# Linear attention and best-two router of a two-layer kernel: value sums with 17-column weights, query features as weights, and match_replace for the two best gates

## The reference

```
q, k, v = x Wq + bq, x Wk + bk, x Wv + bv          # 16 heads of 8
q', k'  = (elu(q R) + 1) / 16, (elu(k R) + 1) / 16 # R: 8 x 32, so 32 features a head
kv      = sum over tokens of k'^T v                # 32 x 8 a head
ksum    = sum over tokens of k'                    # 32 a head
out     = (q' kv) / max(q' ksum, 1e-6)             # then out Wo + bo
gate    = softmax(x Rt)                            # 8 experts; the 2 best are kept
gate    = gate / (sum of the kept + 1e-6)
y       = x W^T + b + sum over experts of gate_e (x A_e^T) B_e^T
```

## Time and profile before

| | us |
|---|---|
| median of three runs | 512.2 |
| the profiled execution | 512.39 |
| its span | 510.6 |
| PE busy | 469.4 |
| DVE busy | 380.0 |
| ACT busy | 241.8 |
| POOL busy | 104.0 |

### The profile page before, as it was taken

How to read it: one execution, slowest core, us unless ns; L and a number is a source line. 1 busy time by engine, 2 the same in 40 slices (tenths; PEclk the granted TensorE clock), 3 DMA queues, 4 the chain that set the end, 5 groups by cost and what they waited for, 6 DMA issues and landing times. The chain is left out here.

```text
span 510.6 us, 8076 instructions
## 1 busy us (share of the span) xinstructions
PE 469.4 (92%) x2949; PEld 233.9 (46%) x2949; DVE 380.0 (74%) x984; ACT 241.8 (47%) x340; POOL 104.0 (20%) x100
## 2 busy tenths in 40 slices
PE   8799989999999999998999899989989998987873
PEld 3332232333433443332435566575656656565552
DVE  6298887887888889879755987854876697664653
ACT  2404746666686665655783122722363236327210
POOL 9790153402480001000010002000200020031020
PEclk9999989999999999999999999968997999899877
DMA  4755342222132243310032113110220011000000
GB/s 154 242 144 186 95 130 94 95 72 80 42 114 95 71 115 106 108 29 13 10 85 57 68 62 104 43 41 20 76 70 22 22 62 42 1 22 0 2 21 21
DMA packets 24867, 36.18 MB, mean 71 GB/s; under 512 B 2678, under 2 KB 16246, under 8 KB 24822
## 3 DMA queue, kind: packets, MB, share of 16 engines
q1 hardware_dynamic: 24828, 35.67, 23.7%
HBM read 23.94 MB, written 11.53 MB: 69 GB/s over the span
## 5 line engine op out<-in xcount | busy, mean ns | idle before, releaser
L1106 DVE TENSOR_REDUCE negmax<-psum 128x1 f32<-128x512 f32 x256 | 170.1, 687 | 37.6 <-PE psum L506 37.4
L810 ACT ACTIVATE probs<-psum 128x1024 f32<-128x1024 f32 x128 | 127.5, 1022 | 62.0 <-PE psum L522 59.8
L506 PE MATMUL psum<-KS,QS 125*128 125x512 bf16 x256 | 99.9, 391 | 8.0 <-DVE negmax L1106 3.6
L541 PE MATMUL psum<-probs,VA 128*32 128x256 f32 x1024 | 81.0, 392 | 0.4 <-ACT probs L810 0.4
L522 PE MATMUL psum<-QS,KS 128*128 128x512 bf16 x256 | 76.5, 382 | 0.3
L789 PE MATMUL psum<-xT,late 128*128 128x512 f32 x144 | 74.0, 639 | 0.0
L506 PEld LDWEIGHTS psum<-KS,QS 125*128 125x128 bf16 x256 | 24.8, 97 | 83.2 <-DVE negmax L1106 39.7
L434 POOL TENSOR_SCALAR var<-mv 128x4 f32<-128x4 f32 x16 | 3.6, 225 | 278.9 <-DVE mv L1006 278.8
L929 ACT ACTIVATE QS<-psum 128x512 f32<-128x512 f32 x36 | 21.6, 599 | 60.1 <-PE psum L789 60.1
L1257 DVE SCALAR_TENSOR_TENSOR QS<-QS,psum 128x512 f32<-128x512 f32 x36 | 24.5, 679 | 31.3 <-ACT QS L929 31.3
L776 PEld LDWEIGHTS psum<-late,QS 128*128 128x128 f32 x288 | 36.6, 195 | 14.9 <-issue 7.3
(11 more groups left out here) (140 smaller groups left out, 568.6 us busy)
## 6 DMA issues: line engine op xcount, KB each, us to landing
stack_dram<-parts SPq DMA_DIRECT2D x24, 384.0 KB, 3.6
cw<-w_dram SPq DMA_DIRECT2D x32, 256.0 KB, 3.2
KS<-stack_dram SPq DMA_DIRECT2D x16, 288.0 KB
QS<-stack_dram SPq DMA_DIRECT2D x16, 288.0 KB
late<-in_late SPq DMA_DIRECT2D x6, 330.5 KB, 4.5
res<-in_x SPq DMA_DIRECT2D x4, 256.0 KB, 3.6
w_dram<-wT SPq DMA_DIRECT2D x4, 256.0 KB, 4.3
out_y<-KS SPq DMA_DIRECT2D x4, 256.0 KB, 2.3
```

Source lines behind the costliest of these rows:

```text
L506: mm(sm_bank(u)[:, :], QS[b % 2][0:KROW, h, qt * P:(qt + 1) * P], KS[b % 2][0:KROW, h, :], start=True, stop=True).then_inc(sm_full, 1)
L541: last_ = mm(ps[6][32 * j:32 * j + 32, q], VA[b % 2][:, kt, h, :], probs[:, n % 2, j, q], start=(kt == 0 and half == 0), stop=(kt == NT - ...
L810: fn(probs[:, n % 2, 2 * hf:2 * hf + 2, :], psum[:, 2 * hf:2 * hf + 2, :], ACT.Exp, scale=float(DH) ** -0.5).then_inc(exp_done, 1)
L1106: V.tensor_reduce(out=negmax[:, G % 4, i:i + 1], in_=sm_bank(u)[:, :], axis=X, op=ALU.max, negate=True).then_inc(sm_free, 1)
```

## The change

V moves from place 6 to 4, Q's steps 2 and 3 from 7 to 6. VK holds, for each pair of heads, 16 values and a column of ones. In KV these 17 columns are the weights, in the four column tiles of the array (one for each group of four heads), and 64 feature columns stream: 32 calls. ACT copies the 128 columns of the sums (kvt), KT transposes them in one go, and DVE writes KVB with 32 masked value columns and 4 masked sum columns a group. O takes a token tile of q features as 128-column weights and streams the 36 columns of KVB; two steps of eight calls, each for two token tiles. Its result has tokens first, with outputs and denominators beside each other, so OT, its ACT copies and the tile OU's use here go. DVE floors, inverts and multiplies once for each step of O. Everything from AT on moves one place forward. KT gets bank 4 behind the experts; Y2 keeps 6, Y1 keeps 4.

The router takes MAX8 of the exponentials into the places 6 to 13 of `top8`, whose places 0 to 5 hold -1, so that places 0 to 7 are six times -1 and the two best; match_replace writes 0 for those two, and the difference to the exponentials is what is kept. The division by the softmax sum is folded into the last one.

```diff
-KVW = HW + 1
+KVW = 2 * DH + 1
+OW = HW + HG
...
-        VK = sb("VK", [P, NT, NG, KVW])
-        KVB = sb("KVB", [P, 2, NG, HW])
+        VK = sb("VK", [P, NT, 2 * NG, KVW])
+        kvt = sb("kvt", [P, P])
+        KVB = sb("KVB", [P, NG, OW])
...
+        top8 = sb("top8", [P, NT, 14])
...
-        steps = ((0, "chunk", 0), (1, "norm1", 0), (3, "x2T", 0), (4, "kp", 0), (4, "qp", 0), (5, "K", 0), (5, "K", 1),
-                 (5, "K", 2), (5, "K", 3), (6, "V", 0), (6, "Q", 0), (6, "Q", 1), (7, "Q", 2), (7, "Q", 3), (7, "KV", 0),
-                 (8, "O", 1), (8, "O", 0), (9, "OT", 1), (9, "OT", 0), (10, "AT", 0), (11, "Y1", 0), (12, "norm2", 0),
-                 (14, "x3T", 0), (15, "lg", 0), (17, "ghT", 0), (18, "Y2", 0), (19, "norm3", 0))
+        steps = ((0, "chunk", 0), (1, "norm1", 0), (3, "x2T", 0), (4, "kp", 0), (4, "qp", 0), (4, "V", 0), (5, "K", 0),
+                 (5, "K", 1), (5, "K", 2), (5, "K", 3), (6, "Q", 0), (6, "Q", 1), (6, "Q", 2), (6, "Q", 3), (7, "KV", 0),
+                 (8, "KT", 0), (8, "O", 0), (8, "O", 1), (9, "AT", 0), (10, "Y1", 0), (11, "norm2", 0),
+                 (13, "x3T", 0), (14, "lg", 0), (16, "ghT", 0), (17, "Y2", 0), (18, "norm3", 0))
...
-                    "V": (vk_done, b + 1), "KV": (kvb_done, b + 1), "O": (sums_done[c % 2], b + 1),
-                    "OT": (floor_done, b + 1) if c else (attn_done, NB * NT + b + 1),
+                    "V": (vk_done, b + 1), "KV": (kvt_done, b + 1), "KT": (kvb_done, b + 1), "O": (attn_done, NB * NT + 2 * b + c + 1),
...
-                if kind == "OT":
-                    pe.wait_ge(sums_done[m], b + 1)
-                if kind == "O" and m == 1:
+                if kind == "KT":
+                    pe.wait_ge(kvt_done, b + 1)
+                if kind == "O" and m == 0:
...
-                    for c in range(4):
-                        for t in range(NT):
-                            last_ = mm(cols(c, KVW), KF[:, t, c * P:(c + 1) * P], VK[:, t, c, :],
-                                       start=(t == 0), stop=(t == NT - 1))
+                    for t in range(NT):
+                        for r in range(2):
+                            for c in range(NG):
+                                at = c * P + 64 * r
+                                last_ = mm(o[32 * c:32 * c + KVW, 64 * r:64 * (r + 1)], VK[:, t, 2 * c + r, :],
+                                           KF[:, t, at:at + 64], start=(t == 0 and r == 0), stop=(t == NT - 1),
+                                           tile_position=(0, 32 * c), skip_group_check=True)
+                if kind == "KT":
+                    last_ = tr(cols(0), kvt[:, :], ident)
                 if kind == "O":
 
-                    for c in range(NG):
-                        last_ = mm(o[HW * c:HW * (c + 1), :], KVB[:, m, c, :], QF[:, b % 2, c, :],
-                                   start=True, stop=True, tile_position=(0, HW * c))
-                if kind == "OT":
-
-                    for t in range(NT):
-                        v = OU[:, 0, m, t * P:(t + 1) * P]
-                        if m:
-                            last_ = mm(cols(t, H), v, ident[:, 0:P:DH], start=True, stop=True)
-                        else:
-                            last_ = tr(cols(t), v, ident)
+                    for t in range(2):
+                        for c in range(NG):
+                            last_ = mm(cols(NG * t + c, OW), QF[:, b % 2, c, (2 * m + t) * P:(2 * m + t + 1) * P], KVB[:, c, :],
+                                       start=True, stop=True)
...
-                if kind == "O":
+                if kind == "KV":
                     wait_full(act, u)
                     if a:
-                        wait_full(act, ("OT", a - 1, m))
-                    fn(OU[:, 0, m, :], bank_of(u)[:, :], ACT.Copy).then_inc(sums_done[m], 1)
+                        wait_full(act, ("KT", a - 1, 0))
+                    fn(kvt[:, :], bank_of(u)[:, 0:P], ACT.Copy).then_inc(kvt_done, 1)
...
-                tot = rl[:, 3, 0:NT]
-                yield from after(V.reduce_sum(tot, e, X))
-                yield from after(V.reciprocal(tot, tot))
-                yield from after(tt(gate8[:, :, :], e, tot.unsqueeze(2).to_broadcast([P, NT, E1]), ALU.mult))
-                m8 = r3(5, 8, rl)
+                tot, picked = rl[:, 3, 0:NT], rl[:, 4, 0:NT]
+                rest, best = r3(5, E1, rl), r3(6, E1, rl)
                 for t in range(NT):
-                    ins = V.max(m8[:, t, :], gate8[:, t, :])
+                    ins = V.max(top8[:, t, 6:14], e[:, t, :])
                 yield from after(ins)
-                yield from top(rl, gate8[:, :, :], m8, 2, E1, 6, "reset8")
-                yield from after(tt(gate8[:, :, :], gate8[:, :, :], r3(6, E1, rl), ALU.mult))
-                yield from after(V.reduce_sum(tot, gate8[:, :, :], X))
-                yield from after(V.tensor_scalar(tot, tot, 1e-6, None, ALU.add))
-                yield from after(V.reciprocal(tot, tot))
-                yield from after(tt(gate8[:, :, :], gate8[:, :, :], tot.unsqueeze(2).to_broadcast([P, NT, E1]), ALU.mult))
+                V.reduce_sum(tot, e, X)
+                for t in range(NT):
+                    ins = V.match_replace(out=rest[:, t, :], in_to_replace=top8[:, t, 0:8], in_values=e[:, t, :], imm_value=0.0)
+                yield from after(ins)
+                yield from after(tt(best, e, rest, ALU.subtract))
+                yield from after(V.reduce_sum(picked, best, X))
+                yield from after(V.scalar_tensor_tensor(out=picked, in0=tot, scalar=1e-6, in1=picked, op0=ALU.mult, op1=ALU.add))
+                yield from after(V.reciprocal(picked, picked))
+                yield from after(tt(gate8[:, :, :], best, picked.unsqueeze(2).to_broadcast([P, NT, E1]), ALU.mult))
...
-                if kind == "KV":
+                if kind == "KT":
                     wait_full(dve, u)
                     if a:
-                        wait_full(dve, ("O", a - 1, 0))
-
-                    kv = bank_of(u)[:, 0:NG * KVW].rearrange("p (c k) -> p c k", k=KVW)
+                        wait_full(dve, ("O", a - 1, 1))
+
+                    kv = bank_of(u)[:, 0:P].rearrange("p (c k) -> p c k", k=32)
                     own = c_["mask"].unsqueeze(1).to_broadcast([P, NG, HW])
-                    tt(KVB[:, 1, :, :], own, kv[:, :, HW:KVW].to_broadcast([P, NG, HW]), ALU.mult)
-                    tt(KVB[:, 0, :, :], kv[:, :, 0:HW], own, ALU.mult).then_inc(kvb_done, 1)
+                    tt(KVB[:, :, HW:OW], kv[:, :, 2 * DH:KVW].to_broadcast([P, NG, HG]), own[:, :, 0:HW:DH], ALU.mult)
+                    tt(KVB[:, :, 0:HW].rearrange("p c (r k) -> p c r k", r=2),
+                       kv[:, :, 0:2 * DH].unsqueeze(2).to_broadcast([P, NG, 2, 2 * DH]),
+                       c_["mask"].rearrange("p (r k) -> p r k", r=2).unsqueeze(1).to_broadcast([P, NG, 2, 2 * DH]),
+                       ALU.mult).then_inc(kvb_done, 1)
                     step(8)
-                if kind == "OT" and m == 1:
+                if kind == "O":
                     wait_full(dve, u)
-
-                    V.tensor_scalar(rt[:, 20, :], bank_of(u)[:, 0:NT * H], 256e-6, None, ALU.max).then_inc(floor_done, 1)
-                    step(1)
-                    dve.wait_ge(floor_done, a + 1)
-                    link(V.reciprocal(rt[:, 21, :], rt[:, 20, :]))
-                if kind == "OT" and m == 0:
-                    wait_full(dve, u)
-                    if a >= 2:
+                    if a >= 2 and m == 0:
                         wait_full(dve, ("AT", a - 2, 0))
-                    tt(attn[:, a % 2, :, :].rearrange("p t (h d) -> p t h d", d=DH),
-                       bank_of(u)[:, :].rearrange("p (t h d) -> p t h d", t=NT, d=DH),
-                       rt[:, 21, :].rearrange("p (t h) -> p t h", h=H).unsqueeze(3).to_broadcast([P, NT, H, DH]),
-                       ALU.mult).then_inc(attn_done, 1)
-                    step(8)
+
+                    v = bank_of(u)[:, 0:2 * NG * OW].rearrange("p (g k) -> p g k", k=OW)
+                    floor, inv = (rt[:, i, 32 * m:32 * (m + 1)].rearrange("p (g h) -> p g h", h=HG) for i in (20, 21))
+                    link(V.tensor_scalar(floor, v[:, :, HW:OW], 256e-6, None, ALU.max))
+                    link(V.reciprocal(inv, floor))
+                    tt(attn[:, a % 2, 2 * m:2 * m + 2, :].rearrange("p t (c h d) -> p (t c) h d", h=HG, d=DH),
+                       v[:, :, 0:HW].rearrange("p g (h d) -> p g h d", d=DH),
+                       inv.unsqueeze(3).to_broadcast([P, 2 * NG, HG, DH]), ALU.mult).then_inc(attn_done, 1)
+                    step(4)
...
+            link(V.memset(top8[:, :, :], -1.0))
```

17 lines of the change are left out of this document (8 added, 9 removed).

## The result

The changed kernel takes 523.29 us (median of 4 runs, 519.18 to 525.75) against 512.75 for the kernel before beside it (511.38 to 518.55): a ratio of 1.0204, 95% interval 1.0159 to 1.0249. It is slower, as forecast, but by 10.5 us and not by 4.3, just past the end of the range (523). A ratio here is taken over executions within 1.5% of the fastest of their kernel, so it is not quite the ratio of the medians. The profiled execution took 525.75 us and is the slowest of the four; its span is 523.0 [before: 510.6, rows 1].

What follows compares the result with a forecast made beforehand. TensorE, busy for 92% of the span, with its clock and the waits on its in-order queue, was taken as the bound. The terms -2.5 - 0.2 + 3.5 + 4.0 - 0.5 = +4.3 us on 512.2 gave 516.5 us, range 506 to 523.

Steps and rivals of the forecast that it cites:

- KV: Value sums on PE: 1.4 us at full clock in place of 3.49, saving 2.1 us a batch, 8.4 in all.
- The rival that the tiles don't overlap: KV's column tiles: 3.4 us in place of 1.4, +2.0 in each of four batches, 524.5 us; chance 0.06.
- O and KT: PE work per batch: new O 3.5 us, KT 0.11, against 3.3 for old O and OT; +0.3, 1.2 in all.
- The KT wait: Beside the experts, O stalls for KVB on VectorE: 1.75 us in each of three batches, +5.2 us; bounds 0 and 3.
- The lg wait: Router logits wait for K's passes on bank 6: 1.3 us in batch 1 (as before), 2.3 in batch 2 (+1.0).
- The down projection's waits: In batch 0, the down projection before O waits 1.8 us for its hidden tile.
- -2.5 - 0.2 + 3.5 = +0.8: Beside the experts: batch 0 gains 2.5 us, batch 1 gains 0.2, batch 2 loses 3.5.
- Batch 0: Slots 14 to 18: gain of 6.1 us at full clock, 1.2 with O at half clock; 2.5 taken.
- the tail: Last batch (3): O starts 1.8 us later behind x2T, z 2.2 us longer behind O; +4.0 us, bounds +1 and +7.
- Router: Shorter chain for the two best gates gives nothing in the last batch; with z's norm wait, -0.5 us taken.
- The rival with half clock in every batch: O at half clock: 3.3 us for each of batches 1 and 2, 2.5 more in the tail; 522.5 us; chance 0.12.

Runs made afterwards that it cites:

- e3: The changed kernel with each step of layer 2 back at the places of the kernel before (V at 6, Q2 and Q3 at 7): 517.47 us, ratio 1.0120.
- e4: The changed kernel plus warming matmuls in the last batch alone, ahead of K2, Q2, KT and O: 515.51 us, ratio 1.0028.
- e1: The kernel before with the new router chain for the two best gates alone: 513.53 us, ratio 1.0005.
- e2: The kernel before with the new KV, kvt and KT alone, O and OT as before: 503.68 us, ratio 0.9811.
- e5: The kernel before with the new O alone, old KV, masks in the new form: 521.94 us, ratio 1.0164.
- e7: The changed kernel with only AT to norm3 put one place later, as before; V and Q stay early: 517.31 us, ratio 1.0080.
- e13: The kernel before with new KV, masks early on VectorE and new O, plus lg's banks taken in turn: 506.74 us, ratio 0.9886.
- e6: The changed kernel with lg and its second half taking the next banks in turn beside the experts: 520.67 us, ratio 1.0170.
- e14: The kernel before with new KV, early masks, new router, last-batch warming and the rule of lg's banks in turn: 492.74 us, ratio 0.9604.
- e15: The kernel before with new KV, early masks, new router, last-batch warming, lg's banks in turn and new O: 500.09 us, ratio 0.9745.
- e8: The kernel before with new KV alone and VectorE writing the masks KVB at KV's place in its list: 494.51 us, ratio 0.9657.

## Why the prediction was right in its direction and wrong in its size

**KV: right, the gain even larger.** 1.02 us at full clock against the 1.4 taken (bounds 0.9 and 3.4). The rival that the tiles don't overlap is dead. The estimate that the prediction worked out from the Trainium skill, TensorEngine Tiling (Array Packing), section Instruction Overhead, was 3.2 us at half clock for 64 short records one behind the other; the trace has 1.91 us at half clock and 1.02 at full, 16 ns from one record to the next, and the measurement decides.

**O and KT: work right, clock mis-sized.** At full clock the 32 records take 3.6 us, as forecast. At half they take 7.05, and that was met in the last batch whole, in batch 0 almost whole and in batch 2 in part (4.86). The timeline of PE in the kernel after, batches 0 and 1:

```profile
339.10 6.42 PE L686 MATMUL psum<-KVB,QS 128*128 128x36 f32 x32 [0.51 <-DVE KVB L969]
...
389.97 3.76 PE L686 MATMUL psum<-KVB,QS 128*128 128x36 f32 x32 [0.61 <-DVE KVB L969]
```

**The KT wait: real, but a third of the size.** 0.51, 0.61 and 0.61 us in place of 1.75. The sum let three 512-column passes of DVE stand ahead of KVB. But KT's slot is always that of a batch's last unit, the shared one, which has two. The timeline of the kernel after shows them, with nothing between them and KVB:

```profile
388.16 0.69 DVE L1257 SCALAR_TENSOR_TENSOR QS<-QS,psum 128x512 f32<-128x512 f32 x1
...
388.94 0.69 DVE L1265 SCALAR_TENSOR_TENSOR QS<-QS,psum 128x512 f32<-128x512 f32 x1
389.54 0.37 DVE L969 TENSOR_TENSOR KVB<-psum,late 128x16 f32<-128x16 f32 x2
```

That made the sum 3.5 us too high there.

**The lg wait: right by size** (1.32 and 2.39 us for 1.3 and 2.3); e3 shows that the banks' turn alone, without the places, makes such a wait.

**The down projection's waits: one foreseen, two not.** That of batch 0 came as forecast, 1.85 us for 1.8. With the norms one place earlier DVE also stands, in the same slot as a unit's passes, waiting for POOL's part of the norm (0.88 us at 361.1), and hands the hidden tile over late: 1.34 and 1.35 us, and 0.57 more for z. One of them on PE:

```profile
364.85 1.16 PE L775 MATMUL psum<-late,QS 128*128 128x128 f32 x8 [1.34 <-DVE QS L969]
```

With x2T's waits for the norm (0.80 and 1.74) these 5.8 us, less the 3.5 that the sum had too much for KVB, are about what the crowded part lost beyond it: 3.1 us where the sum had -2.5 - 0.2 + 3.5 = +0.8. (The other differences nearly cancel.) Batch 0 came out near its forecast by luck. The 2.48 us gap is down to 0.60, and the gate behind O starts at 345.3 (forecast 346.2 at full clock; before 351.0). But O began at 339.1, 3.6 us ahead of its forecast, because the Q steps and KVB were not as late as the sum had them, and then took 6.2 us for 3.5, because the clock fell 0.7 us into it. One gate projection later PE is 4.2 us ahead of the kernel before (350.8 for 355.0) where the sum took 2.5. The prediction also read the slow stretch of the kernel before as 11.5 us from 337.0, where its window began; the clock was at half from 335.0 to 348.6.

**The step that failed: the tail, +4.0 with bounds +1 and +7.** It was +10.1. The step let the clock be at half "over the later part of O and over Y2", some 7 us. It was at half from 469.5 to 496.8, through the LoRA inputs, both pairs of Q, KV, all of O, Y2 and the transpose. The bound had been formed from pieces at half (9 us if all full, 14 if all half, from O on) and priced no half clock ahead of O. There stand two waits of 2.42 us, ahead of K2 (as before) and ahead of Q2 (0.25 before), with the short router matmuls between them. So O came 24.1 us behind x2T where the step had 20.8, and z 14.8 behind O's start where it had 11.8. Filling the waits (e4) gave the clock back and 5.4 us with it. The remaining 4.7 are not the clock: the step had 1.2 us for the same at full clock (1.8 ahead of O, -0.6 behind), e4 shows 3.4 and 1.3, among them the wait for the router's product ahead of KT.

**Router: right**, worth nothing (e1). The -0.5 was put on it and on the wait for z's norm; what stands behind Y1 took 25.1 us for 25.9, which is no test of it.

**Two slips in the prediction's numbers.** The rival with half clock in every batch names 3.7 us for batch 0, but its 522.5 comes out with 1.3, the 2.5 of gain less the 1.2. And the chance of slower adds up to 0.40 + 0.12 + 0.06 = 0.58, not 0.56.

The rival "O at half clock in every batch" (522.5 us) came nearest in its number and was in part right in its mechanism: the clock fell in O in batches 0 and 2 and was at half all through it in batch 3, but batch 1's O ran at full clock, and most of the excess was in the last batch. By the ratios the 10.5 us are made of a gain of 9.7 (new KV, e2), a loss of 8.4 (new O alone, e5), 4.3 for the places (e3; 6.4 by e7), and some 7 that only KV and O together have: e3 is 6.1 us over the kernel before, where the two alone add up to -1.3. Each of these carries 2 to 5 us. Two things come only with both parts. One is the turn of the banks, to which e13 gives 6.1 us. The other is that KT takes the place ahead of the down projection, so that O stands in one piece; the traces speak for it, and no run tests it.

What stays open: whether another bank for O's second half or for Y2 would save Y2's wait of 1.22 us was not tried, nor V and Q moved without the rest, nor, in a kernel with the new KV, the new O in two halves with a down projection between them. That last is the rival to "the new O is dear by itself": beside the experts e5 had it in halves and was 3.0 us shorter than before. Why e6 gained so little where e13 gained 6.1 is only argued from the half-clock spells of one execution each.

## What to carry to other kernels

Count in each step not only PE's time but what it streams: trading long-moving matmuls and transposes for one piece of 32 records that stream 36 columns under full weight loads cost 7.4 us here (e14 to e15) at nearly equal work, while taking such a piece away (KV with 17 columns as weights and 64 streaming) gained 10 us, and 18 with the masks early. Look also at whether such a piece stands whole or is broken by long-moving work. When a step is taken out or added, follow the banks that are given in turn to the next fixed user, and look on the engine that hands tiles over for every wait that now stands ahead of the hand-over. And put a small product that PE waits for ahead of the next unit's passes: that one move (e8) was worth 9.2 us for 4.7 us of waits in three batches.

## What the runs showed of the hardware that was not expected

- Half clock went on for 27.3 us while PE was busy for 21.6 of them (79%), and for 10.3 us from 339.8 with PE busy all the time, while e8's last batch had PE busy for 20.9 of 28.6 us (73%) at 0.94. In e15 the clock fell during O, 2.5 us after its start, with 0.3 us of idle time ahead of it. So PE's busy share alone doesn't tell which way the clock goes.
- Half clock began inside or right behind 32 records of 36 columns under 128-column loads in 21 of 27 cases, and in none of three where a down projection of 0.97 us stood in their middle (e5). That it is the narrow streaming that lets the clock fall is what these traces suggest; no run varies the width alone.
- Four column tiles of 17-column weights, 64 columns streaming in fp32: 64 records in 1.02 us at full clock and 1.91 at half.
- MATCH_VALUE_LOAD takes 0.08 us and MATCH_REPLACE8 0.15, a pair every 0.14 us on 8 elements; four pairs are over in 0.6 us.
- One program's executions differ with their half-clock spells: 519.18 us at a mean clock of 0.952, 523.23 at 0.943, 525.75 at 0.936 (kernel after). The kernel before went from 509.15 to 519.58 in one set of 25 runs, so single executions here tell little under 2%.
